# Loads behind the first turned parts, full-height low-rank products, and a new order of work in a fused attention and feed-forward kernel

## The reference, cut to what matters

```python
x = x + attention(layernorm(x), ctx, ctx)        # 16 batches, 128 rows, width 512
x = x + ffn(layernorm(x))
# attention: q from the normed x, k and v from ctx (width 128); RMS norm with weights, rotary
#   embedding, 16 query heads on 4 key heads of 32, causal softmax, out @ w_out.T
# ffn, on the normed x1:
w_up = (w_up_q - 7.5) * repeat(w_up_scale, 64)   # 2048 x 512 4-bit values held as int32
y1 = x1 @ w_up.T + b_up + x1 @ w_up_lora_a @ w_up_lora_b        # rank 16
x2 = relu(y1)
w_down = (w_down_q - 7.5) * repeat(w_down_scale, 64)            # 512 x 2048
y2 = x2 @ w_down.T + b_down + x2 @ w_down_lora_a @ w_down_lora_b
```

## Time and profile before

| | us |
|---|---|
| median of 3 runs (lowest, highest) | 493.28 (492.91, 493.85) |
| the profiled execution | 493.2 |
| its span, first to last instruction | 491.4 |
| busy: PE, DVE, ACT, POOL | 444.3, 345.7, 302.8, 275.5 |

### The profile page before, as it was taken

How to read it: one execution, slowest core, us unless ns; L and a number is a source line. 1 busy time by engine, 2 the same in 40 slices (tenths; PEclk the granted TensorE clock), 3 DMA queues, 4 the chain that set the end, 5 groups by cost and what they waited for, 6 DMA issues and landing times.

```text
span 491.4 us, 8266 instructions
## 1 busy us (share of the span) xinstructions
PE 444.3 (90%) x2416; PEld 214.7 (44%) x2416; DVE 345.7 (70%) x1075; ACT 302.8 (62%) x927; POOL 275.5 (56%) x308
## 2 busy tenths in 40 slices
PE   0155578999999999999999999999999999999997
PEld 0134434445454545454545454545454444444443
DVE  3959986995959695959595968686777766544341
ACT  1659996775767676666667585857576757461110
POOL 5425788648656675656656574748393927271100
PEclk9998995999999999999999999999999999999999
DMA  6965788447787869776879595979597869565332
GB/s 141 392 127 135 195 232 194 91 95 139 139 156 142 153 139 156 140 156 130 166 119 177 99 192 96 189 114 173 111 173 108 155 118 141 118 87 128 65 73 55
DMA packets 208140, 70.17 MB, mean 143 GB/s; under 512 B 197808, under 2 KB 200496, under 8 KB 207456
## 3 DMA queue, kind: packets, MB, share of 16 engines
q1 hardware_dynamic: 206144, 69.09, 70.5%
q10 hardware_dynamic: 1872, 0.40, 0.5%
q0 software_dynamic: 80, 0.16, 0.1%
HBM read 16.95 MB, written 4.19 MB: 43 GB/s over the span
## 4 chain that ended last, share of the span: by engine, by line
PE 85%; DVE 6%; DMA 3%; ACT 3%; issue 1%; SPq 0%; DVEq 0%; ACTq 0%
PE ff L919 34%; PE ff L933 34%; PE tb L901 8%; PE sb L873 3%; PE tb L889 2%; PE ff L778 2%; DMA wd_lo<-wd_hi 2%; DMA wd_hi<-in_L_xattn_k_norm_w 1%; DVE pr L1176 1%; PE ff L829 1%; ACT pr L675 1%; DVE big L1070 1%; DVE wu_lo L1078 1%; DVE t_sin L1144 0%; ACT wu_hi L632 0%
## 5 line engine op out<-in xcount | busy, mean ns | idle before, releaser
L919 PE MATMUL ff<-wu_hi,xnT 128*128 128x512 f16 x512 | 153.7, 382 | 0.0
L933 PE MATMUL ff<-wd_hi,x 128*128 128x512 f16 x512 | 152.3, 379 | 0.0
L492 POOL TENSOR_TENSOR pr<-pr,rinv 128x512 f32<-128x512 f32 x64 | 73.3, 1145 | 104.3 <-DVE rinv L1086 104.3
L675 ACT ACTIVATE pr<-pr,nmax 128x128 f32<-128x128 f32 x256 | 98.7, 387 | 1.9 <-DVE nmax L1176 1.9
L740 ACT ACTIVATE hid<-z 128x512 f16<-128x512 f32 x64 | 40.2, 628 | 94.6 <-DVE z L1107 94.5
L919 PE MATMUL ff<-wu_lo,xnT 128*128 128x512 f16 x256 | 97.5, 381 | 0.0
L933 PE MATMUL ff<-wd_lo,x 128*128 128x512 f16 x256 | 97.0, 379 | 0.0
L1176 DVE CUSTOM_DVE_ANT_0 pr<-sb,tabs,score_scale 128x128 f32<-128x128 f32 x256 | 73.6, 343 | 23.3 <-PE sb L873 23.2
L1107 DVE SCALAR_TENSOR_TENSOR z<-ff,su,b_row 128x512 f32<-128x512 f32 x64 | 47.8, 746 | 58.5 <-PE ff L919 57.4
L501 POOL TENSOR_TENSOR big<-pr,big 128x512 f16<-128x512 f32 x64 | 76.0, 1198 | 20.8 <-ACT big L706 20.8
L919 PEld LDWEIGHTS ff<-wu_hi,xnT 128*128 128x128 f16 x512 | 48.6, 99 | 59.8 <-issue 7.7
(11 more groups left out here) (147 smaller groups left out, 601.6 us busy)
## 6 DMA issues: line engine op xcount, KB each, us to landing
xt<-in_x SPq DMA_DIRECT2D x16, 256.0 KB, 3.1
big<-in_L_ffn_w_up_q SPq DMA_DIRECT2D x4, 1024.0 KB, 7.5
big<-in_L_ffn_w_down_q SPq DMA_DIRECT2D x4, 1024.0 KB, 5.8
out<-y SPq DMA_DIRECT2D x16, 256.0 KB, 2.1
kvt<-in_ctx SPq DMA_DIRECT2D x16, 64.0 KB, 2.8
wd_lo<-in_L_xattn_w_out SPq DMA_DIRECT2D x1, 1024.0 KB, 7.8
b_row<-in_L_ffn_b_up SPq DMA_DIRECT2D x1, 1024.0 KB, 15.3
pT<-big SPq DMA_TRANSPOSE x64, 3.4
```

The lines of the kernel that those rows point to most:

```text
L492: pool.tensor_tensor(pr[:, m], pr[:, m], rinv[:, p, 4 * m:4 * m + 4].unsqueeze(2).broadcast_to([P, NG, P]), ALU.mult).then_inc(probs, 1)
L675: last = act.activation(pr[:, m, g, :], pr[:, m, g, :], ACT.Exp, bias=nmax[:, p, j:j + 1], scale=-1.0, accum_out=rsum[:, p, j:j + 1])
L919: last = pe.matmul(bank[:], a[:, m, :], b[:, m, 512 * g:512 * g + 512], start=(m == 0 and i == 0), stop=(m == KC - 1 and i == 2))
L933: last = pe.matmul(ff[down_bank[n]][:], x2T[:, part, k + h % HG, :], b[:, h, :], start=(h == 0 and i == 0), stop=(h == HC - 1 and i == 2))
```

## The change

- SyncE: group 1, w_out and batch 1 get slots (369, 242, 106); groups 2 to 7 slots 421 to 1277; batch 2 slot 540; the bias row slot 1233 instead of 7. The rows of factor b (slot 371) then have group 0, batch 1, w_out and group 1 ahead of them, and the turns of queries and keys of batch 0 (399, 414) come next, before group 2.
- All low-rank operands are 128 rows high. Three areas more are cleared, and the copies wait for four clearings.
- Rows and columns of factor a, the down weight and its scales are dealt out to partitions differently (row 4p + i in place of 128 i + p), so turned blocks of down tiles also go to every fourth column, and the loads of scales and factor a have longer runs.
- Start: the norm weights are waited for one by one and their maxima found after the tops; the statistics of batch 0 come after the tops are gathered; the tables are last in ScalarE's DMA queue; GpSimd makes the query tables before the keys of batch 0.
- TensorE issues 64 products of the float16 identity with itself after it has waited for the identity's cast and before it waits for the split factor a. The same helper is called at other places with a count of 0.
- New values of all slot constants; 27 tiles in place of 24 dequantized by VectorE (up tiles 15 both times; the three more are down tiles). Some waits of TensorE stand in another order.

```diff
-R_UP = ((1080, 1861, 2218, 2466), ...
+R_UP = ((1244, 1851, 2165, 2515), (1371, 1888, 2234, 2528), (1516, 1925, 2241, 2543), (1622, 1983, 2280, 2582))
-R_PROJ = (752, 1533, 1994, 2293)
+R_PROJ = (982, 1674, 2009, 2302)
-R_XNTURN = (1167, 1650, 2003, 2293)
+R_XNTURN = (1258, 1729, 2005, 2234)
...
-DVE_TILES = (0, 1, 2, 3, 4, 5, 6, 7, 9, 10, 11, 12, 13, 14, 15, 16, 17, 18, 21, 23, 25, 26, 27, 29)
-LOW_BY_DVE = (2, 3, 6, 7, 8, 9, 10, 14, ... 31)
+DVE_TILES = (0, 1, 2, 3, 4, 5, 6, 7, 8, 9, 10, 12, 13, 14, 15, 16, 17, 18, 19, 20, 22, 23, 24, 25, 27, 28, 30)
+LOW_BY_DVE = (0, 1, 2, 5, 9, 10, 11, 14, ... 31)
...
-LOAD_AT = (3, 282, 526, 863, 944, 1212)
-ROW_LOAD_AT, DOWN_BIAS_LOAD_AT = 7, 1179
-BATCH_LOAD_AT = (2, 777)
+LOAD_AT = (369, 421, 557, 574, 1092, 1168, 1277)
+WO_LOAD_AT = 242
+ROW_LOAD_AT, DOWN_BIAS_LOAD_AT = 1233, 817
+BATCH_LOAD_AT = (106, 540, 1498)
+
+LORA_FILL = 64
...
-LORA_B_ROWS_AT = (83, 737)
+LORA_B_ROWS_AT = (371, 734)
...
-BIAS_ROW_AT = (965, 1355, 1447, 1619)
+BIAS_ROW_AT = (1081, 1180, 1374, 1450)
...
-        a_dn3, a_dn3_late = sb("a_dn3", [R3, H // 2], F16), low_area[0:R3, 3584:4096].bitcast(F16)
+        a_dn3_all, a_dn3_late_all = sb("a_dn3", [P, H // 2], F16), low_area[:, 3584:4096].bitcast(F16)
+        a_dn3, a_dn3_late = a_dn3_all[0:R3], a_dn3_late_all[0:R3]
+        b_dn3_all = high_area[:, 3840:4096].bitcast(F16)
...
-        wdq_v = wdq.rearrange("(j p) (g c) -> g p j c", p=P, c=512)
+        wdq_v = wdq.rearrange("(p j) (g c) -> g p j c", p=P, c=512)
...
+            sp.wait_ge(k_weight_in, 16)
+            sp.wait_ge(q_weight_in, 16)
             load_group(0)
-            sp.dma_start(wo_raw, wo.rearrange("(j p) c -> p j c", p=P)).then_inc(wout_in, 16)
-            load_group(1)
-            load_batch(1)
...
+            def fill(bank, count):
+                for _ in range(count):
+                    pe.matmul(bank[:, 0:P], ident16[:], ident16[:], start=True, stop=True)
...
                 if i == 0:
                     pe.wait_ge(ident_cast, 1)
+                    fill(tb[1], LORA_FILL)
                     pe.wait_ge(a_high, 2)
                     pe.wait_ge(a_low, 2)
...
-                    a, b = (a_dn3[:], a_dn3_late)[t // 24][:, P * (t % 8):P * (t % 8) + P], b_dn3
+                    a, b = (a_dn3_all, a_dn3_late_all)[t // 24][:, P * (t % 8):P * (t % 8) + P], b_dn3_all
...
-                    cols = slice(i, None, 4) if t < UP_TILES else slice(P * i, P * i + P)
-                    last = turn(bank[:, cols], stage[:, g % W_RING, i, P * j:P * j + P],
+                    last = turn(bank[:, i::4], stage[:, g % W_RING, i, P * j:P * j + P],
...
             find_tops()
             norm_powers()
             gather_tops()
+            input_stats(0)
             norm_scales()
```

More of the change, by code:

```diff
@@ L43 @@
[L43 to L47, removed]
@@ L68 @@
[L68 to L73, removed]
+R_STATS = (0, 8, 397, 1356)
+R_SQUARES = (2, 5, 556, 1555)
@@ new lines @@
+R_MOMENTS = (0, 23, 473, 1390)
+R_KEYS = (0, 5, 293, 1861)
+R_POW = (2, 4, 759, 1936)
+R_CENTRE = (3, 49, 653, 1683)
+R_SINES = (2, 100, 544, 1479)
+R_COSINES = (3, 17, 661, 2053)
+R_ROPE = (3, 194, 683, 1491)
+R_KSPLIT = (4, 171, 1051, 1721)
+R_KLOW = (22, 201, 1005, 1486)
+R_KTURN = (414, 630, 1275, 1592)
+R_QSPLIT = (13, 260, 982, 1760)
+R_QLOW = (7, 335, 965, 1506)
+R_QTURN = (399, 627, 1271, 1609)
+R_SCORES = ((53, 499, 1363, 1830), (165, 518, 1473, 1850), (190, 618, 1613, 1870), (255, 824, 1653, 1924))
@@ new lines @@
+R_PLOW = ((405, 1050, 2054, 2417), (446, 1059, 2191, 2455), (503, 1414, 2308, 2597), (522, 1534, 2367, 2615))
+R_PTURN = ((677, 1298, 1741, 1911), (724, 1385, 1757, 1995), (1040, 1422, 1772, 2056), (1046, 1479, 1788, 2070))
+R_VSUM = (466, 790, 1166, 1825)
+R_VARG = (451, 576, 1089, 1717)
+R_VPOW = (526, 688, 1127, 2391)
+R_VSPLIT = (701, 1333, 1813, 2183)
+R_VLOW = (629, 1498, 2199, 2631)
+R_PV = (832, 1586, 1929, 2266)
+R_OHIGH = (808, 1517, 2036, 2336)
+R_OLOW = (647, 1400, 1785, 2110)
+R_PROJ = (982, 1674, 2009, 2302)
@@ new lines @@
+TURN_FILL = (0, 0, 0, 0, 0, 0, 0, 0, 0, 0, 0, 0, 0, 0, 0, 0, 0, 0, 0, 0, 0, 0, 0, 0, 0, 0, 0, 0, 0, 0, 0, 0)
+PV_FILL = (0, 0, 0)
+PROJ_FILL = (0, 0, 0)
+SCORES_FILL = ((0, 0, 0), (0, 0, 0), (0, 0, 0), (0, 0, 0))
+UP_FILL = ((0, 0, 0), (0, 0, 0), (0, 0, 0), (0, 0, 0))
+DOWN_FILL = (0, 0, 0)
+LORA_BHIGH_AT, LORA_BLOW_AT = 7, 5
+LORA_B_ROWS_AT = (371, 734)
+LORA_TURN_AT = (2, 3, 4)
+LORA_COPY_AT = (16, 21, 166)
+WO_ORDER_AT = (45, 51, 52, 99)
+WO_TURN_AT = (183, 212, 363, 374)
+WO_HIGH_AT = (248, 347, 393, 417)
@@ L103 @@
+WO_LOW_AT = (355, 356, 394, 398)
+LORA_A_AT, LORA_ALOW_AT = 6, 4
+BIAS_ROW_AT = (1081, 1180, 1374, 1450)
+WO_SQUARES_AT, WO_SUM_AT, WO_ARG_AT, WO_POW_AT = 41, 5, 83, 87
 RING, W_RING, HID_RING = 4, 3, 3
@@ L409, in _ @@
                         sp.dma_start_transpose(x2T[:, g], hid[:, (4 * n + g) % HID_RING].rearrange("p a h -> p (a h)")).then_inc(x2_turned[g], 16)
-                for g in range(2, 8):
-                    if LOAD_AT[g - 2] == s:
+                for g in range(1, 8):
+                    if LOAD_AT[g - 1] == s:
                         load_group(g)
@@ L420, in _ @@
                                          parts[:, j, :]).then_inc(moved, 16)
-                for n in (2, 3):
-                    if BATCH_LOAD_AT[n - 2] == s:
+                for n in (1, 2, 3):
+                    if BATCH_LOAD_AT[n - 1] == s:
                         load_batch(n)
+                if s == WO_LOAD_AT:
+                    sp.dma_start(wo_raw, wo.rearrange("(j p) c -> p j c", p=P)).then_inc(wout_in, 16)
                 if s == ROW_LOAD_AT:
@@ L877, in products @@
                 if n is not None:
+                    if n == 0:
+                        pe.wait_ge(wo_low, NN)
+                    else:
+                        pe.wait_ge(o_low, n)
+                    if n < FREE:
+                        fill(tb[1], PV_FILL[n])
                     for m in range(NN):
@@ L984, in find_tops @@
                 top(1, s_dn[:].rearrange("p a b -> p (a b)"))
-                dve.wait_ge(norm_w_in, 16 * 2)
-                for j, w in enumerate((qw_bc, kw_bc)):
-                    norm_link(dve.tensor_reduce(wmax[:, j:j + 1], w, AXX, ALU.max, apply_absolute_value=True), wait=False)
                 dve.wait_ge(b_flat_in, 16 * 2)
@@ L997, in norm_powers @@
             def norm_powers():
+                dve.wait_ge(q_weight_in, 16)
+                dve.wait_ge(k_weight_in, 16)
+                for j, w in enumerate((qw_bc, kw_bc)):
+                    norm_link(dve.tensor_reduce(wmax[:, j:j + 1], w, AXX, ALU.max, apply_absolute_value=True), wait=False)
                 dve.wait_ge(norm_scale_steps, 2)
```

151 lines of the change are left out of this document (66 added, 85 removed).

## The result

| | before | after |
|---|---|---|
| median (lowest, highest) | 493.25 (492.91, 493.85) | 486.42 (486.13, 486.77), 4 runs |
| ratio, 95% interval | | 0.9861 [0.9843, 0.9878] |
| the profiled execution, its span | 493.2, 491.4 | 486.36, 484.6 |
| last down part of batch 0 starts | 112.58 | 104.52 |
| last work of TensorE ends | 488.14 | 481.30 |

The change makes the kernel 6.8 us faster. The time predicted was 486.0, with a range of 481.5 to 490.8.

The account below looks back on a forecast made before the run. VectorE's weight preparation was taken to set when TensorE becomes full, after which TensorE alone bounds the kernel. The last down part 7.15 us earlier, other terms 0: 493.2 - 7.15 = 486.0 us, range 481.5 to 490.8.

Parts of the forecast that it names:

- The rows: Factor b's rows, SyncE's queue: issued at 19.9, landed at 24.0 us instead of 29.60, closing VectorE's 5.43 us gap.
- VectorE's sum: Scales to tile 31: 17.5 + 83.5 work + 4.5 idle = 105.5; last down part at 105.6, 7.15 us earlier.
- The hole at 82.3: VectorE's 3.04 us wait for the first up product, 82.30 to 85.41, claimed to go as that product starts earlier.
- TensorE's sum: Input turned near 69 us plus 29 us of work gives 98, 7 us ahead of VectorE, not setting the end.
- the height of the operand: Down tiles' turns, 48 to 128 rows with new columns: 0.26 us a tile, 2.6 us over 10 tiles, counted as 0.
- the clock: TensorE's clock fall in 75.56 to 84.40 held back some 4.3 us; if repeated, 102 instead of 98; counted as 0.
- The products: 64 identity products at the start: 7.7 us, cost 0 to 1.3, gain bound -0.8, both hidden; taken as 0.
- A: Preparation stretch: new order fits better, waits of 1.5 instead of 4.5, scales 1 us sooner; 482.0 us; chance 0.17.
- B: Bias row and group 6 come late, ScalarE stops, tiles 20 to 31 slip by 4; 490.0 us; chance 0.15.
- C: Factor b's rows land no earlier, small packets being slow by themselves; 5.4 us of gain gone; 491.4; chance 0.08.
- D: Repeating part: a batch waits on TensorE, 1 us over 12 batches; slower, 498 us; chance 0.07.
- E: Loads behind the turned parts arrive late, gap only moves from 26 to 31 us; 493 us; chance 0.05.

Follow-up runs that it names:

- e1: Kernel before with the bias row and batch 2 issued behind the first turned keys: 488.11 us, ratio 0.9905.
- e4: Kernel after with group 2, batch 2 and the bias row put back ahead of the rows of factor b: 488.28 us, ratio 0.9907.
- e3: Kernel before with 128-row operands in the down tiles' low-rank products, columns left as they were: 489.32 us, ratio 0.9932.
- f2: Kernel after with the down tiles' low-rank products 48 rows high again: 488.60 us, ratio 0.9915.
- f1: Kernel after without the 64 identity products: 485.54 us, ratio 0.9849.
- e2: Kernel before with group 2, batch 2 and the bias row all behind the first turned keys: 490.06 us, ratio 0.9949.
- g3: Kernel after, unchanged, measured once more for the spread of its own time: 486.20 us, ratio 0.9857.
- g1: Kernel before with bias row and batch 2 behind the first turned keys, plus 128-row low-rank operands for the down tiles: 485.38 us, ratio 0.9829.
- f4: Kernel after with batch 5's load moved behind the turn of batch 1's normed rows on SyncE's queue: 485.42 us, ratio 0.9862.

## Why the prediction was right, and where only the total was

**The rows.** Right in kind. The issue was at 21.43, not 19.9 (the low parts of factor b end only at 21.37), and the first tile at 25.49, not 24. By then the bytes in front no longer counted: from 20 to 22 us the queues moved 16 and 0 GB/s, and the rows landed a median of 2.6 us after their issue, so their issue sets when they land. That the first tile came 1.5 us late cost VectorE nothing, as said: it had five dequantizations until 28.8. By e1 the bias row and batch 2 behind give 4.8 us in the old order; by e4 against after these two and group 2 give only 1.9 in the new.

**VectorE's sum.** Forecast 17.5 + 83.5 + 4.5 = 105.5; measured 18.7 + 82.3 + 3.4 = 104.4. The scales were 1.2 us later, just past the bound of 1: the tops' last maximum ended 1.2 us sooner (9.54 against 10.78), but the maxima of the norm weights (0.87) now stand behind it, the powers took 1.19 us in place of 0.40 ahead of the spreading, and the statistics of batch 0 (0.68) follow on the chain. The work was 1.2 us less counted from there, and the leftover waits 1.1 less. The hole at 82.3 closed though the first up part came only at 72.74, not near 69.

**TensorE's sum: the step that failed.** I gave TensorE 7 us to spare and put the height of the operand and the clock at 0. Measured at either side, the 48 rows cost 3.6 us in the old order (e3) and 2.2 in the new (f2 against after), the clock's part not told apart in either. The row that says it was in front of me: from 85.41 to 111.50 TensorE was busy 26.09 of 26.09 us, and 3.11 of 3.11 just before, while VectorE had 24.67 and 0.07. An engine that is never idle up to the point that sets the end is not 7 us ahead of it. I read that stretch by VectorE's last low part. But this lay ready at 111.55, and the last down part started at 112.58, because TensorE was still at the third. I then added TensorE's new sum from an estimate of the first up part (69, measured 72.74) and a tidy list behind it (29 us, measured 31.8 with some 1.5 idle). The two sums are not independent either: the turned input, issued at 68.01, had landed in 3.1 us, but TensorE was waiting until 71.42 for VectorE's low part of a tile ahead of it. In the new kernel VectorE's sum ends at 104.4 and TensorE's, counted from 72.74 without its 1.5 us of idle time, at 103.0. That the total came out is partly luck: VectorE's sum, which I did work out, is close to the end of the stretch once TensorE has lost the 2.6 us of its ten tiles. That is argued from the sums, not shown by a run.

**What is given back.** The forecast had nothing late behind the last down part. 1.24 us are, for the input turn of batch 1. The misses nearly cancel: the last down part came 8.06 us earlier where 7.15 were forecast, 0.9 more, and 1.2 were given back, hence 486.4 for 486.0. (The 112.75 of the prediction is a sum from the chain of waits; in TensorE's timeline, where the 104.52 stands, the part starts at 112.58.)

**The products.** In the trace nobody waits for them, which bears out a cost of 0, but f1 is 0.9 us lower and the intervals overlap, so the time leaves it open. The gain was within its bound and is 0. By the busy time, 64 took 6.14 us and not 7.7, so the later ones ran at the higher of the two levels; but the first tiles' turns took 1.11, 1.06, 0.70 and 0.60 us all the same, and the granted clock of 26.00 to 31.43 is 0.75. Between lie 5.9 us (19.57 to 25.49) in which TensorE had only the factor's 20 turns and two sums. The Trainium skill (TensorE: Matmul & The Clock Gate, Part 1: The HAM clock gate) says that idling takes the full rate back; this trace agrees.

**The rivals.** A (waits of 1.5 us, scales sooner): waits were 3.4 and scales later. B (the bias row late): it was issued at 60.48 and landed in 9.2 us, at 69.7, and ScalarE scaled it at 70.49 without stopping. C fell with e1. D (a batch waits in the repeating part): 372.32 of 372.40 us busy. E (the gap only moves): it happens in the old order (e2), not in the new.

**Still open.** Within one kernel the runs of the changed forms spread over 0.6 to 6 us (after 0.6, g3 1.9, g1 3.2, f4 5.8), those of the kernel before over 1.6 beside f4 and 2.5 beside g1. In the profiled runs the clock falls in other places: the clock in tenths in 40 slices of 12.1 us, from the page of g1 and of g3:

```profile
PEclk9998999999999999999999999999999999999999
```

```profile
PEclk9986699999999999999999999999999999999999
```

Where it falls behind 60 us it costs TensorE time in the stretch that sets the end: with one and the same kernel TensorE is busy 38.95 us at a clock of 0.96 (g3) and 38.36 at 1.00 (after) from 60 to 105 us, and f4's profiled run shows it in the last down part. What makes it fall in one run and not in another, no experiment here tells, and edits of under 1 us can't be settled against it.

## What to carry to other kernels

Before an engine is called ahead of the path, look at its idle time up to the point that sets the end: one that is busy 26.09 of 26.09 us has no slack, whatever a sum from a guessed start says. Small loads that work waits for belong in front of bulk loads in the queues (4.65 us in e1, where the bytes made 3.4), and what is moved behind must still have cover (e2). Undo each part of a large reordering alone: here two edits of a few lines in the old order (g1) reach what the whole change reaches.

## What was not expected of the hardware

- A product of 128 x 512 with operands 48 rows high takes no longer by itself (0.39 against 0.38 us), but with the four 128-row turns behind it the tile takes 0.91 us instead of 0.65. The timeline of TensorE's weight loads shows where, in f2 and then in the kernel after. With 48 rows the loads of product and turns start only with their own product (82.86, 83.18), 0.42 and 0.23 us after the load before; with 128 rows the product's load starts at 79.71 ahead of its product at 79.93, and the turns' first load beside that product:

```profile
82.86 0.09 PEld L850 LDWEIGHTS ff<-wd_hi,wd_lo 48*128 48x128 f16 x1 [0.42 <-issue]
83.18 0.42 PEld L791 LDWEIGHTS ff<-tabs,big 128*128 128x128 f32 x4 [0.23 <-issue]
```

```profile
79.71 0.10 PEld L850 LDWEIGHTS ff<-wd_hi,wd_lo 128*128 128x128 f16 x1
79.93 0.57 PEld L791 LDWEIGHTS ff<-tabs,big 128*128 128x128 f32 x4
```

- The last of three small copies of rows took 9.25 us to land with group 2, the bias row and batch 2 (2.4 MB) just in front and 4.81 with the bias row and batch 2, 1.38 MB, gone (e1). 1.38 MB less in 4.44 us less are 310 GB/s, so these two cost a third more than the 408 GB/s of the earlier trace rows say, while group 2 costs what its bytes say (e2). Which of the two it is, or group 2's earlier issue, is not shown.
- The granted clock went to the higher level at 18.6 us, during the 64 products, and back to the lower at 25.4, as the first tile began. Ahead of 18.6 the profile has no entry and shows 1.00, but the products' pace tells the level: 12 in 17.40 to 18.40, 18 in 18.60 to 19.57. The 1.00 at the start of the kernel before is to be read with the same care, as four turns took 1.06 us there and 0.60 later. And the clock falls in other places from run to run of one kernel (after and g3).
